# Summing the weighted states of a selective scan token-major, by transposes that add in PSUM

## The reference

```python
def _mamba(u, in_w, conv_w, conv_b, xp_w, dt_w, dt_b, A_log, Dp, out_w):
    xz = u @ in_w.T                      # 256 -> 2 x 512 channels
    x, z = jnp.split(xz, 2, axis=-1)
    xpad = jnp.pad(x, ((0, 0), (D_CONV - 1, 0), (0, 0)))
    xc = conv_b + sum((xpad[:, k:k + L, :] * conv_w[:, k] for k in range(D_CONV)))
    x = jax.nn.silu(xc)
    xdbl = x @ xp_w.T                    # -> dt (16), B (16), C (16)
    dt = jax.nn.softplus(xdbl[..., :DT_RANK] @ dt_w.T + dt_b)
    ...
    dA = jnp.exp(dt[..., None] * A)
    dBx = (dt * x)[..., None] * Bm[:, :, None, :]
    # h = dA * h + dBx along the tokens; ys = sum over the 16 states of h * C
    y = jnp.swapaxes(ys, 0, 1) + x * Dp
    y = y * jax.nn.silu(z)
    return y @ out_w.T
```

## Time and profile before

| | us |
|---|---|
| median of 3 runs | 5985.66 |
| lowest and highest | 5982.96, 5986.95 |
| the profiled execution | 5982.95 |
| its span in the profile | 5981.3 |
| POOL busy | 5274.7 |
| DVE busy | 5264.1 |
| PE busy | 5193.1 |
| ACT busy | 3354.3 |

### The profile page before, as it was taken

One profiled execution on the slowest core, in us unless ns is written; L12 is line 12 of the kernel. 1 busy time (PEld: TensorE's weight loads), 2 busy tenths in 40 slices (PEclk: granted clock), 3 DMA queues, 4 the chain that ended last, 5 costly groups with the idle time before them and its releaser, 6 DMA issues. The chain is left out here.

```text
span 5981.3 us, 47174 instructions
## 1 busy us (share of the span) xinstructions
PE 5193.1 (87%) x14366; PEld 2599.2 (43%) x14366; DVE 5264.1 (88%) x4001; ACT 3354.3 (56%) x5046; POOL 5274.7 (88%) x2694
## 2 busy tenths in 40 slices
PE   6968898988989888898878898988989888898889
PEld 5824444444444444444334444444444444444344
DVE  3469999999999999999969999999999999999900
ACT  0055666656666565666555666656666565666511
POOL 0069999999999999999969999999999999999900
PEclk9989999999999999999989999999999999999999
DMA  4133323233232322323123323232232322323164
GB/s 154 71 112 96 102 66 108 69 102 91 77 108 63 106 85 85 109 63 105 59 82 99 98 70 108 69 102 87 80 109 63 105 80 91 108 61 108 59 217 141
DMA packets 220338, 563.65 MB, mean 94 GB/s; under 512 B 27842, under 2 KB 94274, under 8 KB 218532
## 3 DMA queue, kind: packets, MB, share of 16 engines
q1 hardware_dynamic: 204276, 533.89, 28.7%
q10 hardware_dynamic: 15808, 26.75, 1.2%
HBM read 500.43 MB, written 60.58 MB: 94 GB/s over the span
## 5 line engine op out<-in xcount | busy, mean ns | idle before, releaser
L909 POOL TENSOR_TENSOR dbx<-dtx,b_all 128x896 f32<-128x896 f32 x1792 | 3705.9, 2100 | 0.2
L665 PE MATMUL mamba_ps<-hc,ident 128*128 128x448 f32 x7168 | 3152.6, 575 | 627.1 <-POOL hc L916 613.6
L735 ACT ACTIVATE mamba_ps<-dt,w 128x448 f32<-128x448 f32 x3584 | 2135.2, 629 | 1617.4 <-DVE hc L848 1298.8
L665 PEld LDWEIGHTS mamba_ps<-hc,ident 128*128 128x128 f32 x7168 | 1376.5, 199 | 2183.1 <-issue 1231.4
L841 DVE TENSOR_TENSOR_SCAN mamba_ps<-mamba_ps,dbx 128x896 f32<-128x896 f32 x1120 | 2254.0, 2013 | 52.8 <-ACT mamba_ps L735 50.7
L916 POOL TENSOR_TENSOR hc<-hc,c_all 128x896 f32<-128x896 f32 x672 | 1409.0, 2097 | 0.0
L841 DVE TENSOR_TENSOR_SCAN hc<-mamba_ps,dbx 128x896 f32<-128x896 f32 x672 | 1353.8, 2015 | 52.5 <-ACT mamba_ps L735 52.0
L848 DVE TENSOR_TENSOR hc<-mamba_ps,c_all 128x896 f32<-128x896 f32 x1120 | 1216.1, 1086 | 77.8 <-DVE mamba_ps L841 2.0
L628 PE MATMUL mamba_ps<-u,w 128*128 128x448 f32 x1792 | 803.0, 574 | 59.0 <-DVE skip L858 25.7
L628 PEld LDWEIGHTS mamba_ps<-u,w 128*128 128x128 f32 x1792 | 363.7, 205 | 437.0 <-issue 336.8
L818 DVE SCALAR_TENSOR_TENSOR x<-mamba_ps,w,x 128x440 f32<-128x440 f32 (+2 forms) x672 | 436.5, 650 | 16.4 <-ACT x L749 15.8
(11 more groups left out here) (95 smaller groups left out, 2182.2 us busy)
## 6 DMA issues: line engine op xcount, KB each, us to landing
b_all<-bc_scratch SPq DMA_DIRECT2D x448, 448.0 KB, 6.6
c_all<-bc_scratch SPq DMA_DIRECT2D x448, 448.0 KB, 6.1
u<-u_scratch SPq DMA_DIRECT2D x58, 448.0 KB, 8.7
y_scratch<-ytok SPq DMA_DIRECT2D x56, 448.0 KB, 3.2
src<-y_scratch SPq DMA_DIRECT2D x56, 448.0 KB, 4.6
xb<-in_x SPq DMA_DIRECT2D x4, 3136.0 KB, 11.8
u_scratch<-ub ACTq DMA_DIRECT2D x28, 448.0 KB, 8.1
src<-in_x SPq DMA_DIRECT2D x28, 448.0 KB, 6.8
```

What stands on the lines that cost most here:

```text
L665: last = nc.tensor.matmul(y_ps[j % 2], ident[:, :], hc[g % HC_RING][:, e * T:(e + 1) * T], start=False, stop=(g == GP - 1 and e == 1))
L735: last = nc.scalar.activation(decay[g % 2][:, e * T:(e + 1) * T], blk(dt[s.par], j), ACT.Exp, scale=w[:, c:c + 1])
L909: nc.gpsimd.tensor_tensor(view(dbx[g % BX_RING], 0, [[T, 2], [1, T]]), view(dtx[s.par], j * T, [[0, 2], [1, T]]), view(b_all, 2 * g * T, [ ...
```

## The change

In `mambas`:

- **The sums.** `hc` becomes the stationary operand, in chunks of 112 tokens, and the identity moves: 8 transposes a slot that add in PSUM, in place of 2 matmuls (4 instructions). The sum of a block is then tokens by channels, 112 partitions by 4 x 128. The skip term becomes 4 matmuls with `x` as the stationary operand.
- **The way back.** ACT copies a block's finished sum to a new tile `ytr` (`take_y`), PE transposes it back into a work bank (`turn_back`, 4 transposes, items `y0` to `y3`), and DVE gates from that work bank.
- **The order.** `SCHEDULE` has 19 items in place of 15. `x1`, `x2`, `x3` are earlier, `z0` to `z3` come after the `dt` items, silu of `z` moves from slot 27 to slot 3 of the tile that uses it, and the taps and gates move with them. In the front at the start of a pass, `z0` to `z3` all stand between `dt3` and the softplus; silu of `z` is no longer in that front.
- **The tile loop** is written over absolute tile numbers. A copy of one tile of `u` within DRAM, at the stage's start, goes away with the wait for it.

```diff
 SCHEDULE = {
-    "x0": (0, 2), "x1": (2, 5), "out0": (5, 7), "x2": (9, 10), "out1": (9, 11), "x3": (12, 13), "z0": (13, 14),
-    "z1": (16, 17), "z2": (17, 18), "xp": (18, 19), "dt0": (19, 20), "dt1": (20, 21), "dt2": (21, 22), "dt3": (22, 23),
-    "z3": (23, 25),
+    "x0": (0, 2), "x1": (2, 3), "x2": (5, 6), "x3": (7, 8), "y3": (10, None), "out0": (13, 14), "out1": (15, 16),
+    "y0": (16, None), "xp": (18, 19), "dt0": (19, 20), "dt1": (20, 21), "dt2": (21, 22), "dt3": (22, 23), "y1": (23, None),
+    "z0": (24, 25), "z1": (26, 27), "z2": (27, 28), "z3": (28, 29), "y2": (30, None),
 }
-SILU_X_AT, SOFTPLUS_AT, SILU_Z_AT = 16, 24, 27
+SILU_Z_AT, SILU_X_AT, SOFTPLUS_AT = 3, 16, 24
-GATE_AT = {16: 0, 23: 1, 29: 2}
-LAST_GATE_AT = 3
+TAKE_Y_AT = {4: 3, 12: 0, 20: 1, 28: 2}
+GATE_AT = {11: 3, 16: 0, 24: 1, 31: 2}
...
-        y_ps = [bank(4)[:, 0:T], bank(5)[:, 0:T]]
+        y_ps = [bank(4)[0:TCH, :], bank(5)[0:TCH, :]]
...
-                sp.dma_start(u_dram[TILES], u_dram[0]).then_inc(u_wrapped, 16)
-                sp.wait_ge(u_wrapped, 16)
...
-                        nc.tensor.matmul(y_ps[j % 2], skip[:, j * 128:(j + 1) * 128], blk(x[s.par], j), start=True, stop=False)
+                        for c in range(4):
+                            nc.tensor.matmul(y_ps[j % 2][:, c * 128:(c + 1) * 128], x[t % 2][:, j * T + c * TCH:j * T + (c + 1) * TCH],
+                                             skip[:, j * 128:(j + 1) * 128], start=(c == 0), stop=False, skip_group_check=True)
...
-                        last = nc.tensor.matmul(y_ps[j % 2], ident[:, :], hc[g % HC_RING][:, e * T:(e + 1) * T],
-                                                start=False, stop=(g == GP - 1 and e == 1))
+                        for c in range(4):
+                            ins = nc.tensor.matmul(y_ps[j % 2][:, c * 128:(c + 1) * 128], hc[g][:, e * T + c * TCH:e * T + (c + 1) * TCH],
+                                                   ident[:, :], start=False, stop=(g == GP - 1 and e == 1), is_transpose=True,
+                                                   skip_group_check=True)
...
+                def turn_back(t, j):
+                    pe.wait_ge(ytr_ready, DB * t + j + 1)
+                    b = take(Item(t, f"y{j}"))
+                    for c in range(4):
+                        ins = nc.tensor.matmul(b[:, c * TCH:(c + 1) * TCH], ytr[j % 2][:, c * 128:(c + 1) * 128], ident[0:TCH, 0:TCH],
+                                               start=(c == 0), stop=(c == 3), is_transpose=True, skip_group_check=True)
+                    ins.then_inc(work_ready, 1)
...
+                def take_y(t, j):
+                    act.wait_ge(sums_done, SLOTS * t + GP * (j + 1))
+                    if DB * t + j >= 2:
+                        act.wait_ge(work_ready, Item((DB * t + j - 2) // DB, f"y{(j - 2) % DB}").ready())
+                    nc.scalar.copy(ytr[j % 2][:, :], y_ps[j % 2]).then_inc(ytr_ready, 1)
...
-                    nc.vector.tensor_tensor(blk(sz[par], j), y_ps[j % 2], blk(sz[par], j), ALU.mult).then_inc(yg_ready, 1)
+                    it = Item(t, f"y{j}")
+                    dve.wait_ge(work_ready, it.ready())
+                    ins = nc.vector.tensor_tensor(blk(sz[t % 2], j), work[it.slot][:, 0:T], blk(sz[t % 2], j), ALU.mult)
+                    ins.then_inc(work_free[it.slot], 1)
```

More of the change, by code:

```diff
@@ L527, in mambas @@
[L527 to L555 removed]
+                return self.c // 2
@@ L557, in mambas, with upto @@
+        def upto(eng, signal, count):
+            if count > 0:
+                eng.wait_ge(signal, count)
+        first = lambda t: t % TILES == 0
+        last = lambda t: t % TILES == TILES - 1
         with nc.Block() as block:
@@ new lines, in out_proj @@
+                def out_proj(t, i):
+                    it = Item(t, f"out{i}")
+                    b = take(it)
+                    for h in range(2):
+                        c = 2 * i + h
+                        for j in range(DB):
+                            ins = nc.tensor.matmul(b[0:TCH, h * FEAT:(h + 1) * FEAT],
+                                                   sz[t % 2][:, j * T + c * TCH:j * T + (c + 1) * TCH],
+                                                   w[:, W_OUT + j * FEAT:W_OUT + (j + 1) * FEAT], start=(j == 0), stop=(j == DB - 1))
+                    ins.then_inc(work_ready, 1)
@@ L778, in before @@
-                def before(m):
-                    act.wait_ge(w_ready, m * 16 + 16)
-                def front(f):
-                    for n in range(SLOTS):
-                        front_slot(f, n, wait_x=False)
-                def step(s, i):
-                    for n in range(SLOTS):
-                        decays(s, n)
-                        for name in due(1, n):
-                            if name in OUTS and not s.first:
-                                out_copy(s, 0, int(name[-1]), s.item(name))
-                        if not s.last:
-                            front_slot(s.front(), n)
-                    if s.last:
-                        for i in range(2):
-                            out_copy(s, 1, i, s.item(f"end{i}"))
@@ new lines, in _ @@
+                nc.vector.memset(dtr[:, :], 1.0).then_inc(ones_set, 1)
+                for t in range(2 * TILES):
+                    if first(t):
+                        dve.wait_ge(w_ready, t // TILES * 16 + 16)
+                        for j in range(DB):
+                            nc.vector.tensor_scalar_mul(skip[:, j * 128:(j + 1) * 128], ident[:, :], w[:, W_D + j:W_D + j + 1]).then_inc(skip_ready, 1)
+                        for j, back in TAP_AT.values():
+                            conv_tap(t, j, back)
+                    for n in range(SLOTS):
+                        scan(SLOTS * t + n)
```

545 lines of the change are left out of this document (259 added, 286 removed).

## The result

The changed kernel takes 6076.6 us (median of 4 runs, 6075.3 to 6078.7), the kernel before 5984.9 in runs beside it. The ratio is 1.0154, with a 95% interval of 1.0136 to 1.0171: it is slower by 1.5%, where 5993 was forecast. The profiled execution has a span of 6074.9 us.

The account below looks back on a forecast made before the run. POOL was taken to bound the kernel at 94.2 us a tile, so 0 inside tiles; pass starts +1.9 and +3.9 and ends +1.0 made +6.8 on the median 5985.66, rounded 5993, range 5983 to about 6010.

Parts of the forecast that it names:

- What bounds: Inside the tiles POOL sets 94.20 us; DVE could do a tile in 92.95, leaving 1.25 us of free waits.
- Part 1: Sums as transposes: 0.96 us a slot for 1.57, PE loses 1093 us of work, worth 0 inside a tile.
- Half or less of 3152.6: Sign to look for: PE's sums fall to half or less of 3152.6 us at the full clock.
- Part 2: ACT's copies, 2.3 us a tile; waits for `take_y` and `turn_back` taken as 0, up to 1 us at low clock.
- Part 3: Order within a tile: 0.47 us of wait goes, 0.3 comes in slot 16; DVE's waits 1.1 us a tile.
- Part 4: Starts of the passes, outside POOL's cover: +1.9 us in the first pass, +3.9 in the second.
- Part 5: Ends of the passes: -1.1 us each, up to +9.9 at half clock; taken as +0.5 per pass.
- Rival A: Inside tiles, low PE clock delays items for ACT and DVE takes over from POOL: 53 us, 6046; chance 0.24.
- Rival B: Transposes do not raise PE's clock, PE at 1.2 GHz throughout: 126 us a tile, 7780; chance 0.03.
- Rivals C and D: C: a gain from faster POOL or DVE, 5957, chance 0.03. D: low clock at pass edges, +12 to +40, 6008, chance 0.12.

Follow-up runs that it names:

- e7: The changed kernel with both edits: ACT takes `out1` out in slot 17, behind silu of `x`, and the softplus stands ahead of `z0` to `z3`; 5983.4 us.
- e10: The kernel with both edits (e7), with its sums as plain matmuls, twice PE's work for them; 6052.1 us.
- e3: The changed kernel with the sums run as plain matmuls of the same shape, two instructions for each transpose; 6070.8 us.
- e1: The changed kernel with ACT taking `out1` out in slot 17, behind silu of `x`, in place of slot 16; 6001.4 us.
- e2: The changed kernel with DVE gating block 3 of the previous tile in slot 10 in place of slot 11; 6032.5 us.
- e4: The changed kernel with only the second half of each slot's states summed, 4 transposes a slot in place of 8; 6070.5 us in a single run.
- e12: The changed kernel with PE making `out1` in slot 14 in place of 15, ACT's order unchanged; 6002.4 us.

## Why the prediction was wrong

**What bounds.** Right: POOL's 94.2 us a tile and DVE's 92.95 behind it. e7 gives POOL's floor, and the changed kernel, e10 and e3 give DVE's tile plus its waits.

**Part 1, the sums.** The price was right: 28672 plain instructions at nearly full clock took 3417.7 us in e3, 0.12 each, and the changed kernel's 14336 took 2096.9, 0.15 each at a granted 0.87. "Half or less of 3152.6" did not fit that price: 0.96 for 1.57 us a slot is 61%, and measured were 67%. Worth 0 in a tile: right in e7, though e10 shows that a tile doesn't forgive twice the work. The clock fell to 0.87, just above the 0.7 to 0.85 forecast.

**Part 2, the copies and waits.** `take_y` never waited inside a tile, and the gate never waited for `turn_back`. But the gate's place mattered: once DVE was late, PE stood idle for 1.51 us ahead of `out0` for it, and `out0` came at the low clock.

**Part 3, the order within a tile.** This step failed. I charged ACT's slot 16 with the copy of `out1`, 0.58 less a margin of 0.27, and did not ask when PE would have `out1` ready. I priced the waits of ACT for `take_y` and for `x1`, and left this one out. It measured 1.40 us, plus 0.59 for the copy, ahead of 4.3 us of silu and table loads: 2.23 us of DVE's wait and not 0.3. With it DVE waits 2.6 us a tile where 1.25 are free, and 1.38 us is paid in nearly every tile, the 75 us that e1 gives back. The rest of the sum held: in e7, where `out1` is out of the way, the waits are 1.2 us for the 1.1 forecast. The room can be counted. At the full clock the two projections and the sums of two slots take 8.8 us (597.15 to 605.98). In the third tile this left 0.14 us to the end of ACT's decays of slot 16; in a late tile there are 9.3 us from the end of the gate (1557.17) to the end of these decays (1566.45), so 8.8 would just have fitted. At the low clock `out0` takes 1.8 us more, and the chain came to 10.6. So two things together make the loss: an order with next to no room for `out1`, and a clock that is low behind PE's pause ahead of `out0`. I had charged up to 2 us a tile for a low clock, by way of `x1` and `take_y`, and asked it of neither `out0` nor `out1`.

**Part 4, the starts.** The sum was +1.9 and +3.9; measured are +8.7 and +6.8. The term that failed most is `z0` to `z3`. In the first pass the softplus began 10.5 us after ACT's last take-out of `dt`, and before the change 1.3 us after it: +9.2, and +8.2 in the second pass, for +6.2. That is between the price at the full clock and the 12.4 at half clock, since in the first pass half of them ran at each. `dt0` to `dt3` took 5.34 us for 3.40 in the first pass, +1.9 for nothing, and 4.76 for 5.17 in the second, -0.4 for -1.8. `xp` took 4.90 for 3.18, +1.7 for +2, and 5.98 in the second pass, +2.8. `xp` began 4.2 us earlier in the first pass, for 6.3. Of these the part of the copy of `u` can't be read from one execution: the loads began at 315.56 in the changed kernel and between 312.5 and 318.3 in the others, for 316.96 before.

**Part 5, the ends.** Measured +0.2 at the end of the kernel, and from the last sums to the first copy of `out` at the first pass's end 10.9 us for 10.8, for +0.5 each: nothing to mend. The sums took 5.09 us for 6.28, where I had 3.9.

**The rivals.** Rival A is what happened, with its mechanism: PE's clock is low, an item comes late to ACT, ACT holds the decays behind it, and DVE takes over. Its price was near too: at 2.2 us of waits it gave 6046; the 0.4 us more are 22 us in 56 tiles, and the starts cost 10 more than forecast, which makes 6078. But the items that it named, `x1`, `xp` and `dt`, are late in the changed kernel only in single tiles, and in e2. The late item was `out1`. What I set against it, that PE busy without a break gets its clock back, did not hold where it was needed: in e2's slow tile PE was busy for 8.00 of 8.00 us at a granted 0.52.

Rival B is refuted: the granted clock was 0.87. The Trainium skill, TensorE: Matmul & The Clock Gate, Part 4: PE-mode transpose, holds that the full clock does not engage for transposes. The traces here disagree for float32: with half of the transposes of the sums left out (e4) the clock of the tile was 0.73 and with all of them 0.87. Rivals C and D did not come.

What stays open: what first put `out0` of the fourth tile at a granted 0.83, and why the low clock in e2 comes in some tiles only. That the loop needs the low clock on `out0` is read from single tiles and from three edits that cut it in three places (e1, e2, e12); no run holds the clock at 1.00 with these sums and this order. Nor is the wait for the gate the only way to a low clock there: in e2, where PE never waits for it, `out0` still took 5.3 us in five tiles of the first pass. With both edits a tile takes 94.29 us for 94.19 before, some 6 us in all, which I traced to nothing.

## What to carry to other kernels

When items move in an in-order queue, price not only each moved item but the moment at which its producer is done, and then what stands behind the consumer: an item that is taken out just ahead of 4 us of table loads and silu passes any lateness on in full. Ask also whether the lateness comes back to the producer: here a late DVE made the next `out1` late, and the traces show one slow tile followed by slow ones to the end of the pass. Read the first tiles of a pass and not only a tile from its middle. Find the engines' slack first (1.25 us a tile here), and hold every new wait against it. Work saved on an engine that nobody waits for is worth nothing, but check with a run that doubles its work whether this holds in every stretch.
